# Eight waits of VectorE for h, each contained in another wait of the same operation, left out ahead of its loop

## The reference

```
h  = relu(layernorm(x))
H  = (adj != 0);  xw = h @ W1.T
m  = Be * (H.T @ xw);  out = Dn * (H @ m) + b1      # Dn, Be: inverse weighted / plain degrees
r  = layernorm(relu(out)) * gamma + beta
x1 = x + h + (second hypergraph convolution of r with W2, b2)

g  = relu(layernorm(x1))
e  = leaky_relu(sj + si + ab);  A = adj * exp(e);  T = A / rowsum(A)
out = x1 + relu(sum over k of (T^k g) @ Wk[k] + bk[k])
```

## Time and profile before

| | |
|---|---|
| median of 3 runs | 823.91 us |
| profiled execution | 824.95 us |
| its span, first to last instruction | 823.2 us |
| TensorE busy | 806.8 us (98%) |
| VectorE busy | 640.3 us (78%) |
| ScalarE, GpSimd busy | 474.6 us (58%), 429.6 us (52%) |
| granted TensorE clock, mean | 0.997 |
| instruction packets, queues q14 and q8 | 40 and 17 |

### The profile page before, as it was taken

One profiled execution on the slowest core, in us unless ns is written; L12 is line 12 of the kernel. 1 busy time (PEld: TensorE's weight loads), 2 busy tenths in 40 slices (PEclk: granted clock), 3 DMA queues, 4 the chain that ended last, 5 costly groups with the idle time before them and its releaser, 6 DMA issues.

```text
span 823.2 us, 16671 instructions
## 1 busy us (share of the span) xinstructions
PE 806.8 (98%) x5750; PEld 751.5 (91%) x5750; DVE 640.3 (78%) x1740; ACT 474.6 (58%) x1005; POOL 429.6 (52%) x588
## 2 busy tenths in 40 slices
PE   7989999999999999999999999999999999999998
PEld 6878999999899989989899998998989999899997
DVE  6989878876878767878678787787877878786676
ACT  4438366572845728367383754747456483664745
POOL 2676573634738355482545736365473645832242
PEclk9999999999999999999999999999999999999999
DMA  9411204041130402204022130312204022020001
GB/s 299 124 64 52 91 15 153 2 137 32 42 124 0 166 2 76 89 0 166 2 76 90 33 133 2 121 45 76 89 2 160 6 76 90 13 91 1 26 2 52
DMA packets 39881, 58.03 MB, mean 70 GB/s; under 512 B 2576, under 2 KB 21008, under 8 KB 39824
## 3 DMA queue, kind: packets, MB, share of 16 engines
q1 hardware_dynamic: 39104, 57.42, 20.9%
q10 hardware_dynamic: 720, 0.01, 0.0%
HBM read 49.03 MB, written 8.39 MB: 70 GB/s over the span
## 4 chain that ended last, share of the span: by engine, by line
PE 85%; DVE 6%; issue 4%; POOL 2%; ACT 1%; DMA 1%; ACTq 0%; SPq 0%; DVEq 0%; POOLq 0%
PE ps L810 79%; PE ps L1035 3%; PE ps L965 1%; DVE x L1456 1%; PE ps L1011 1%; DVE y L1399 1%; DMA adj_sb<-in_adj 1%; DVE st_x L1462 1%; DVE inc L1222 1%; DVE part_a L1228 1%; DVE st_r L1331 1%; ACT h_f L591 0%; POOL skip L414 0%; POOL h_hi L402 0%; DVE mv_x L1281 0%
## 5 line engine op out<-in xcount | busy, mean ns | idle before, releaser
L810 PE MATMUL ps<-w_hi,part_a 128*128 128x256 f32 (+1 forms) x512 | 157.6, 342 | 6.8 <-DVE part_a L1228 4.2
L421 POOL TENSOR_TENSOR y<-y,bk_row 128x256 f32<-128x256 f32 x64 | 56.6, 914 | 199.3 <-DVE a_lo L1355 190.4
L810 PE MATMUL ps<-w_lo,part_a 128*128 128x256 f32 (+1 forms) x384 | 122.5, 319 | 0.0
L810 PEld LDWEIGHTS ps<-w_hi,part_a 128*128 128x128 f32 x512 | 96.2, 188 | 22.4 <-DVE part_a L1228 6.9
L810 PE MATMUL ps<-wk_hi,xt_hi 128*128 128x258 f32 (+1 forms) x256 | 89.4, 349 | 0.1
L810 PE MATMUL ps<-wk_hi,xt_lo 128*128 128x258 f32 (+1 forms) x256 | 86.7, 339 | 0.0
L810 PE MATMUL ps<-wk_lo,xt_hi 128*128 128x258 f32 (+1 forms) x256 | 86.6, 338 | 0.0
L810 PEld LDWEIGHTS ps<-w_lo,part_a 128*128 128x128 f32 x384 | 72.7, 189 | 5.4
L1349 DVE TENSOR_TENSOR e_sb<-e_sb,adjt_sb 128x512 f32<-128x512 f32 x64 | 44.2, 692 | 40.3 <-ACT e_sb L673 40.3
L810 PE MATMUL ps<-w_hi,part_b 128*128 128x256 f32 x256 | 72.4, 283 | 0.0
L488 POOL TENSOR_TENSOR xt_lo<-xl,xt_hi 128x256 fp32r<-128x256 f32 x60 | 56.1, 964 | 30.4 <-ACT xt_hi L747 30.4
(11 more groups left out here) (161 smaller groups left out, 2530.9 us busy)
## 6 DMA issues: line engine op xcount, KB each, us to landing
adj_sb<-in_adj SPq DMA_DIRECT2D x30, 512.0 KB, 5.9
adjt_sb<-in_adj_t SPq DMA_DIRECT2D x15, 1024.0 KB, 5.3
xin<-in_x SPq DMA_DIRECT2D x15, 512.0 KB, 4.6
out_dram<-x SPq DMA_DIRECT2D x15, 512.0 KB, 3.3
w_row<-in_adj SPq DMA_DIRECT2D x16, 256.0 KB, 3.5
adjt_sb<-in_adj_t SPq DMA_DIRECT2D x4, 256.0 KB, 7.1
e_sb<-in_w_t SPq DMA_DIRECT2D x2, 512.0 KB, 8.4
y<-in_wk SPq DMA_DIRECT2D x3, 256.0 KB, 7.0
```

The source lines that it names most:

```text
L421: pool.tensor_tensor(y10[:, t, D:], y10[:, t, D:], bk_row[:, :], ALU.add).then_inc(po_y0, 1)
L810: return pe.matmul(dst, stationary, moving, start=first, stop=last, skip_group_check=True)
```

## The change

The wait of VectorE for ac_hf is left out of `h_lo_of`, which is called eight times, four times in each of the steps -1 and 0. The wait for h_hi_made stays, and is now the operation's own; the eight records fall away, all ahead of the loop. VectorE's program has 860 records, and its loop's are 285 to 568. No other engine's program changes, and nothing in the loop does.

```diff
                 def h_lo_of(t):
 
-                    wait(dve, ac_hf, at(s, 1, t))
                     wait(dve, h_hi_made, at(s, 1, t))
                     dve.tensor_tensor(h_lo[:, t, :], h_f[:, t, :], f32(h_hi[:, t, 0:D]),
                                       ALU.subtract).then_inc(h_lo_made, 1)
```

## The result

The changed kernel takes 819.17 us (median of six runs, 818.90 to 819.42), the kernel before 824.41 us beside it (six runs, 823.74 to 825.42): a ratio of 0.994, with a 95% interval of 0.993 to 0.995. The change makes it faster by 5.2 us.

What follows compares the result with a forecast made beforehand. TensorE's work was taken as the floor, with VectorE's branch stalls lengthening five steps. 824.95 - 5.81 - 0.07 = 819.07 us for the profiled execution; for the median, 818.5 between 818.03 and 819.07, range 817.2 to 820.0.

Steps and rivals of the forecast that it cites:

- What bounds the kernel: TensorE's work is the floor; five steps entered by VectorE's loop branch take 0.8 to 1.6 us longer.
- Pages of 128 records with edges at 192, 320, 448, 576: VectorE's program lies in 128-record pages; entering one orders the next; the old loop's branch, record 576, began a page.
- entering 576 orders the fifth page: At VectorE's loop branch: reaching record 576, not jumping, orders page E, which pushes out the loop's first page A.
- The buffer holds four pages: VectorE's instruction buffer: four pages of 128 records stay, so the moved loop needs no packets in later turns.
- The gain: The five steps behind VectorE's branch fall to 49.27 us each: 5.81 us, with outer bounds 0 and 17.4 us.
- The eight records themselves: Wait records ahead of h_lo in steps -1 and 0: 0.07 us gained, at most 0.56 us.
- The loss of up to 4.3 us by VectorE and GpSimd slowing each other: Steps -1 and 0: engines brought closer together might collide, 4.3 us outer bound, taken as none; within the slower 4%.
- That of a buffer with three pages: Rival at VectorE's loop branch: the head is still missed, no change, 823.84 us; no-change rivals 9% in all.
- The one on the slow side, a second stall at the loop's start: Rival: a page edge between records 285 and 293 makes VectorE stall twice a turn, 841 us; slower rivals together 4%.
- Reading ahead beyond the edge: Rival at the branch seven records before 576: VectorE enters the next page in some turns, 821 us; 5%.

Runs made afterwards that it cites:

- the run with 20 records: Changed kernel with all eight waits out and 20 wait records (40 waits) in VectorE's step 1, loop 305 to 588: 824.71 us, 1.0007 to the kernel before.
- the runs with 7 and 35 records: Changed kernel, all eight waits out, 7 or 35 wait records in VectorE's step 1 (loop 292 to 575, 320 to 603): 818.77 us and 819.03 us.
- the one with one wait left out: Kernel before with only the first h_lo wait of step -1 left out, seven kept, loop 292 to 575: 819.08 us, 0.9939.
- 8, 20 and 34 records: Changed kernel, all eight waits out, 8, 20 or 34 wait records in VectorE's step 1: 823.92, 824.71 and 831.76 us.
- the run with 34 records: Changed kernel with all eight waits out and 34 wait records (68 waits) in VectorE's step 1, loop 319 to 602: 831.76 us, 1.0088 to the kernel before.

## Why the prediction was right

**What bounds the kernel.** Right. The five long steps were the whole of the gain: 5.8 us by the steps, and the spans differ by 823.2 - 817.5 = 5.7.

**Pages of 128 records with edges at 192, 320, 448, 576.** Right to the record at two of them: 575 or 576 as the branch's place, and 319 or 320 as the loop's first record, each decides between fast and slow. The edge at 448 rests on its packet alone and the one at 192 on the spacing. The prediction placed the branch at the exit between 698.81 and 698.94, a little late: the trace has it at 698.6, as it has the first one at 200.1, and the packet is 0.7 us behind it in both places. The step from the packet at the exit to "entering 576 orders the fifth page" is borne out by the run with 20 records: there 576 is entered 12 records ahead of the branch. Its instruction packets in 196.8:196.9 and in 200.7:200.8 are these:

```profile
q14 instruction: 1, 0.01, 32.0%
q14 instruction: 1, 0.01, 30.8%
```

The first is the edge's, some 3 us ahead of the branch at 199.68; the second is the branch's own, 1.0 us behind it, and none comes 0.6 to 0.7 us behind.

**The buffer holds four pages.** This was the open step. No row of the kernel before told four pages from three; the prediction took four from a stated size and because three would be an odd one, not from a row. It holds: four pages a turn stay (the kernel after, the runs with 7 and 35 records, the one with one wait left out), five don't (before, 8, 20 and 34 records). The Trainium skill, "Runtime: NRT & Kernel Launch", section "Instruction fetch mechanics", gives 512 instructions for such an engine, and these runs agree: 4 x 128. What the Trainium skill says there of two lines of 16 KiB, 256 instructions each, these runs do not bear out: 40 packets of 0.33 MB are 8 KB each, one for each 128 records, and a loop of 284 records stays as long as it touches three pages.

**The gain.** 5.81 us were worked out for the profiled execution, 5.88 with the eight records; it gained 824.95 - 819.3 = 5.65 and the medians 5.24. For the median the prediction had two values, 818.03 and 819.07, and took 818.5 between them; 819.17 was measured. So the second was nearer, by which the 1.04 us that the profiled execution has above the median lie in the stalls. The spread of the runs agrees: 1.7 us before (823.74 to 825.42) and 0.5 us after (818.90 to 819.42). The price of a stall isn't one wait alone. TensorE's timeline in the kernel before shows a second one, some 30 us behind the branch at about 399:

```profile
429.76 0.39 PE L810 MATMUL ps<-w_hi,part_a 128*128 128x256 f32 x1 [0.34 <-DVE part_b L1342]
```

Laid beside the kernel after, product by product, TensorE falls back by 0.7 to 1.0 us at the first product that needs L1228 in each of the five steps, and by another 0.1 to 0.6 here and there behind. That is why the steps cost between 0.8 and 1.6. I had the sum from the steps, so this did not touch it.

**The eight records themselves.** 0.07 us was forecast. At L1395 in step 1 the kernel after is 0.08 us earlier than the one before (96.60 and 96.68). The runs can't tell that from nothing. The loss of up to 4.3 us by VectorE and GpSimd slowing each other did not come.

**The rivals.** That of a buffer with three pages fell with the result. The one on the slow side, a second stall at the loop's start, did not come in the changed kernel, but its mechanism is real: the run with 34 records shows it. I had priced it at 3.5 us a turn; against before it cost 831.76 - 824.37 = 7.4 us in five turns, 1.5 each. The second page takes 2.25 us to come, not 3.5; the first record comes 2.8 us behind the branch, not 3.5, and the branch itself 0.4 us earlier; and some 3.3 of the 7.4 us are the clock's. The three steps without the lower clock are 51.3 us on average, against 50.4 for the five of the earlier trace rows, so that the second stall by itself cost some 0.9 us a turn. Reading ahead beyond the edge is excluded down to one record.

## What to carry to other kernels

Where a loop of an engine is longer than two pages of its program, count the pages that one turn touches, the branch included, and add the one that is fetched ahead: if these are more than the buffer holds (four here), every branch back stalls, and moving the loop by a few records takes that away where it makes the count one less. "Issue" time on one engine right behind a loop's branch, instruction packets that come in each turn, and steps that are longer at every second place are what to look for in a profile. Once it is seen, an edit ahead of the loop should be judged by where it leaves the loop, since one record moved this kernel by 0.6% and no instruction of the loop changed.

## What the runs showed of the hardware that I had not expected

A missing page is ordered 1.0 us behind the branch, and the first record of it runs 2.8 to 2.9 us behind the branch (runs with 34 and 20 records). When an edge's own order goes just ahead, it is 3.5 to 3.8 us (before, and with 8 records). The next page is ordered only as the missing one is entered, so a branch into the last records of a page pays twice (2.8 + 2.3 us with one record left, 2.9 + 0.8 with fifteen, 3.5 + 0 with twenty-seven). And of the five waits of 1.7 to 1.9 us for which TensorE idled in the run with 34 records, two were followed by a granted clock at its lower level, while none of the waits of 0.6 to 0.8 us at the branches of the kernel before was.
